# A decoder layer with a mixture of experts: the first expert's last token tile computed for all its tokens, and the down bias as one product of 72 stacked rows

## The reference

```python
logits = h @ router_weight.T + router_bias
top_vals, top_idx = jax.lax.top_k(logits, 2)
scores = zeros.at[token, top_idx].set(softmax(top_vals))        # T x 8
gate_up = einsum('th,ehj->etj', h, gate_up_proj) + gate_up_proj_bias
gate, up = minimum(gate_up[..., ::2], 7), clip(gate_up[..., 1::2], -7, 7)
act = (up + 1.0) * gate * sigmoid(1.702 * gate)
expert_out = einsum('eti,eih->eth', act, down_proj) + down_proj_bias
out = einsum('te,eth->th', scores, expert_out)
```

## Time and profile before

| what | value |
|---|---|
| median of 3 runs | 865.51 us (865.01 to 867.3) |
| profiled execution | 868.43 us, its span 866.6 us, mean granted clock 0.98 |
| PE busy | 840.4 us, 97% |
| DVE busy | 478.0 us, 55% |
| ACT busy | 319.1 us, 37% |
| POOL busy | 97.1 us, 11% |
| DMA | 97.39 MB, mean 112 GB/s |

### The profile page before, as it was taken

How to read it: one execution, slowest core, us unless ns; L and a number is a source line. 1 busy time by engine, 2 the same in 40 slices (tenths; PEclk the granted TensorE clock), 3 DMA queues, 4 the chain that set the end, 5 groups by cost and what they waited for, 6 DMA issues and landing times.

```text
span 866.6 us, 12600 instructions
## 1 busy us (share of the span) xinstructions
PE 840.4 (97%) x4913; PEld 735.6 (85%) x4913; DVE 478.0 (55%) x875; ACT 319.1 (37%) x718; POOL 97.1 (11%) x92
## 2 busy tenths in 40 slices
PE   7999999999999999999999999999988999999996
PEld 6989898989899898978799878888867888888883
DVE  4435445363635463485860343455576677777756
ACT  4443324242333433342352222122233365555434
POOL 0000000000000000000000000110221144443431
PEclk9999999999999999999999999999975999999998
DMA  9990634514030003003110001110287366665235
GB/s 326 341 283 20 204 132 143 189 56 147 6 98 6 25 8 122 1 6 133 50 36 1 4 33 36 61 49 13 63 327 222 126 201 182 190 197 156 53 68 182
DMA packets 35759, 97.39 MB, mean 112 GB/s; under 512 B 6665, under 2 KB 9225, under 8 KB 33009
## 3 DMA queue, kind: packets, MB, share of 16 engines
q1 hardware_dynamic: 32224, 88.69, 30.5%
q0 software_dynamic: 3472, 7.87, 4.5%
HBM read 64.10 MB, written 31.53 MB: 110 GB/s over the span
## 4 chain that ended last, share of the span: by engine, by line
PE 87%; DVE 6%; ACT 3%; issue 2%; DMA 1%; POOL 0%; POOLq 0%; SPq 0%; DVEq 0%
PE bank L315 69%; PE bank L696 3%; PE bank L730 3%; PE bank L625 3%; PE bank L789 2%; PE bank L684 1%; PE bank L1066 1%; DVE w_gu L1421 1%; DVE prob L1468 1%; PE bank L974 1%; PE bank L602 1%; PE bank L768 1%; PE bank L807 1%; ACT prob L1128 1%; DVE x_g L1421 1%
## 5 line engine op out<-in xcount | busy, mean ns | idle before, releaser
L315 PE MATMUL bank<-w_kv,cT 128*125 128x512 f32 x576 | 143.5, 400 | 0.0
L315 PE MATMUL bank<-xT,w_qkv 128*128 128x512 f32 (+1 forms) x672 | 137.8, 365 | 0.2 <-ACT qT L1118 0.2
L315 PEld LDWEIGHTS bank<-xT,w_qkv 128*128 128x128 f32 x672 | 122.1, 188 | 15.2 <-ACT qT L1118 0.5
L315 PEld LDWEIGHTS bank<-w_kv,cT 128*125 128x125 f32 x576 | 104.2, 186 | 23.7
L315 PE MATMUL bank<-x_g,w_gu 128*128 128x288 f32 x768 | 111.3, 304 | 3.4 <-DVE x_g L1421 2.9
L315 PEld LDWEIGHTS bank<-x_g,w_gu 128*128 128x128 f32 x768 | 107.2, 194 | 5.1 <-issue 3.2
L499 POOL TENSOR_TENSOR ln_rs<-ln_ve,half 128x1 f32<-128x1 f32 (+2 forms) x16 | 11.3, 710 | 629.3 <-DVE ln_ve L1550 614.8
L315 PE MATMUL bank<-w_o,zT 128*128 128x512 f32 x336 | 79.8, 395 | 0.5 <-DVE acc L1756 0.5
L315 PE MATMUL bank<-w_qkv,xT 128*128 128x256 f32 x588 | 77.3, 287 | 0.0
L315 PEld LDWEIGHTS bank<-w_o,zT 128*128 128x128 f32 x336 | 61.7, 188 | 15.0 <-DVE acc L1455 1.8
L315 PEld LDWEIGHTS bank<-w_qkv,xT 128*128 128x128 f32 x588 | 72.2, 191 | 0.0
(11 more groups left out here) (169 smaller groups left out, 1207.5 us busy)
## 6 DMA issues: line engine op xcount, KB each, us to landing
x_rows<-blank SPq DMA_DIRECT2D x9, 2084.0 KB, 16.1
raw_gu<-in_w_gu_dram SPq DMA_DIRECT2D x8, 2048.0 KB
raw_w<-in_w_qkv_dram SPq DMA_DIRECT2D x22, 512.0 KB, 8.6
raw_dn<-in_w_down_dram SPq DMA_DIRECT2D x8, 1024.0 KB, 8.9
raw_c<-in_ctx_t_dram SPq DMA_DIRECT2D x8, 750.0 KB, 4.3
raw_o<-in_w_o_dram SPq DMA_DIRECT2D x8, 512.0 KB, 4.4
xg<-x_rows SPq DMA_DIRECT2D x8, 512.0 KB, 6.7
raw_kv<-in_w_kv_dram SPq DMA_DIRECT2D x2, 1024.0 KB, 6.8
```

Source lines behind the costliest of these rows:

```text
L315: last = nc.tensor.matmul(mm_out, lhs(a, k), rhs(b, k), start=(k == 0 and i == 0), stop=(k == n - 1 and i == 2))
```

## The change

The last token tile (tile 6, `END`) does not send rows to expert 0 any more. Instead expert 0 is computed for all 128 tokens of this tile, token-wise on the partitions, and added with each token's score for expert 0 (zero where it didn't choose it). In the scatter, the slots of tile 6 that belong to expert 0 go to a part of `x_rows` that nobody reads, and tile 6 is not counted for expert 0. So expert 0's rows are complete after the scatter of tile 5, and SP reads them then; the load of `raw_gu[1]` stands behind that read, and the reads of experts 1 and 2 wait for the scatter of tile 6 (`end_out`).

The computation for tile 6 is: `end_gate_up`, three blocks of 8 products with 512 columns, for the three pairs of parts, each behind a piece of the old routing work, and two products of one row for the bias; `end_clamp`, `end_swish`, `end_hidden` on tiles of 128x512; `end_turn`, four transposes; `end_h_high`, `end_h_low`; `end_down`, 12 products of 512 columns, behind expert 0's gate/up; `end_add` into `acc`. `base_store(6)` waits for `end_add`.

With it the order of the experts changes: down of expert 0 now follows `end_down` directly, before gate/up of expert 1, and nothing stands between gate/up of experts 1 and 2. Expert 1's gate/up matrix is split wholly at the end of expert 0; expert 0's down matrix in its second and third quarter. `SPLITS` for expert 2's matrix is as before.

The down bias is one product a tile in place of three: scores are written three times in `score3` at rows 0, 32 and 64 of a 72-row stack, and the bias three times in `dn_b`, the middle one holding the low part of the bias and the last group of the scores the low part of the scores.

The rest of the diff merges semaphores (`bn_ok` into `mv_ok`, `ri_ok` into `rz_ok`, `level_ok` into `put_ok`, `rest_ok` into `made`, `id_ok` into `slot_ok`), with the same waits.

```diff
@@ banks and order of the last stretch
-            last = [("rk", 4), ("st", 0), ("t1", 5), ("rt", 5), ("t1", 6), ("rk", 5), ("rt", 6), ("db", 0), ("rk", 6),
-                    ("cnt", 0), ("db", 1), ("db", 2), ("st", 1), ("db", 3), ("db", 4), ("db", 5), ("db", 6)]
+            last = [("rk", 4), ("st", 0), ("t1", 5), ("rt", 5), ("db", 0), ("rk", 5), ("t1", 6), ("rt", 6), ("db", 1),
+                    ("rk", 6), ("st", 1), ("db", 2), ("db", 3), ("db", 4), ("db", 5), ("db", 6), ("cnt", 0)]
...
-        SPLITS = {0: ((3,), (), (), (), ()), 1: ((), (), (), (0,), (1, 2, 3))}
+        SPLITS = {0: ((), (), (), (), (0, 1, 2, 3)), 1: ((), (), (), (0,), (1, 2, 3))}
@@ SP
-            sp.wait_ge(*ready("wo", NT - 1))
-            sp.dma_start(raw_gu[1], t["w_gu"][1]).then_inc(in_gu[1], 16)
...
-            sp.wait_ge(row_out, 16 * 2 * NT)
-            for e in range(3):
+            sp.wait_ge(row_out, 16 * 2 * END)
+            rows_in(xg[0], 0, in_xg[0])
+            sp.wait_ge(*ready("wo", NT - 1))
+            sp.dma_start(raw_gu[1], t["w_gu"][1]).then_inc(in_gu[1], 16)
+            sp.wait_ge(end_out, 16 * 2)
+            for e in range(1, 3):
                 rows_in(xg[e], e * ROWS, in_xg[e])
@@ PE, last stretch
             cross_out(6)
             turn_x2(5)
             router(5)
+            down_bias(0)
+            rank(5)
             turn_x2(6)
-            rank(5)
             router(6)
-            down_bias(0)
+            end_gate_up(0, 0)
+            down_bias(1)
             rank(6)
-            count()
-            down_bias(1)
+            pe.wait_ge(m["end_dve"], 1)
+            end_gate_up(1, 0)
+            for h in range(2):
+                nc.tensor.matmul(banks[END_BANK[h]][:, :], all_ones[0:1, :], bias_end[0:1, h * D:(h + 1) * D], ...)
+            turn_scores(1)
             down_bias(2)
-            turn_scores(1)
-            for n in range(3, NT):
-                down_bias(n)
+            down_bias(3)
+            down_bias(4)
+            down_bias(5)
+            pe.wait_ge(m["gu_lo"], KC)
+            end_gate_up(0, 1).then_inc(m["end_mm"], 1)
...
-            for k in range(3):
-                gather(0, k)
+            gather(0, 0)
+            gather(0, 1)
+            down_bias(6)
+            count()
+            gather(0, 2)
@@ PE, experts
                     gate_up_part(e, w_gu[e % 2], x_g[e % 2], q)
-                    if e == 0 and q + 1 < KC:
-                        gather(1, q)
-                    if q and e and e + 1 < NE:
+                    if e == 0 and q == 0:
+                        end_turn()
+                        for k in (4, 5, 7):
+                            pe.wait_ge(free[k], LAST[k])
+                    if q and e + 1 < NE:
                         gather(e + 1, q - 1)
                 if e == 0:
-                    for k in range(6, 8):
-                        pe.wait_ge(free[k], LAST[k])
-                else:
+                    end_down()
+                if e != 1:
                     for k in range(3):
-                        down(e - 1, k)
+                        down(max(e - 1, 0), k)
@@ DVE, last stretch (new order)
+            choose(5)
             x2_norm(6)
-            choose(5)
             assign(5)
+            bias_add(0)
             choose(6)
+            split_lo(x_end[:, 1], x2T[:, END % 2], x_end[:, 0]).then_inc(m["end_dve"], 1)
             assign(6)
+            gu_low(0, 0, 0)
             bias_add(1)
-            gu_low(0, 0, 0)
+            gu_low(0, 0, 1)
             scores_low(1)
+            gu_low(0, 0, 2)
+            gu_low(0, 0, 3)
             bias_add(2)
...
+            gather_low(0, 0)
+            gather_low(0, 1)
+            bias_add(3)
+            gather_low(0, 2)
+            end_clamp()
+            bias_add(4)
+            end_hidden()
             bias_add(5)
             bias_add(6)
-            for k in range(3):
-                gu_low(1, 1, k)
+            levels()
@@ DVE, experts
-                    if q == 1 and not more:
+                    if q == 1 and not more or q == 2 and e == 0:
                         dn_low(e, e % 2)
                 hidden(e, KC - 1)
...
                 for k in splits_at(e, KC):
                     gu_low(e + 1, (e + 1) % 2, k)
+                    if e == 0 and k == 1:
+                        end_add()
-                if more:
+                if e and more:
                     dn_low(e, e % 2)
```

More of the change, by code:

```diff
@@ L423, in _ @@
             sp.dma_start(raw_gu[0], t["w_gu"][0]).then_inc(in_gu[0], 16)
+            with nc.allow_non_contiguous_dma(reason="one expert's bias as a row"):
+                sp.dma_start(bias_end[0:1, :].rearrange("o (c p) -> o c p", p=P),
+                             t["gu_b"].rearrange("p e c -> e c p")[0:1]).then_inc(in_bias, 16)
             sp.dma_start(raw_dn[0], t["w_down"][0]).then_inc(in_dn[0], 16)
@@ L1710, in _ @@
                 .then_inc(m["gub_ok"], 1)
+            nc.vector.memset(score3[:, :, :], 0.0)
             nc.vector.memset(csum[:, 0, :], 0.0).then_inc(m["csum_ok"], 1)
@@ L1736, in _ @@
             wo_low(p)
+            dve.wait_ge(m["wo_lo"], NP_)
+            nc.vector.memset(raw_dnb, 0.0).then_inc(m["ones_col"], 1)
             divide(p)
@@ L1857, in _ @@
             cross_stats(6)
+            choose(5)
             x2_norm(6)
[L1859 removed]
             assign(5)
+            bias_add(0)
             choose(6)
+            dve.wait_ge(m["end_act"], 1)
+            split_lo(x_end[:, 1], x2T[:, END % 2], x_end[:, 0]).then_inc(m["end_dve"], 1)
             assign(6)
[L1863 to L1865 removed]
@@ L1874, in _, with levels @@
             bias_add(1)
-            gu_low(0, 0, 0)
+            gu_low(0, 0, 1)
             scores_low(1)
+            gu_low(0, 0, 2)
+            gu_low(0, 0, 3)
             bias_add(2)
-            gu_low(0, 0, 1)
-            bias_add(3)
-            gu_low(0, 0, 2)
-            bias_add(4)
-            gu_low(0, 0, 3)
+            def levels():
+                dve.wait_ge(*ready("cnt", 0))
+                nc.vector.tensor_reduce(most[:, 0:1], bank("cnt", 0)[:, 0:NE], AX.X, ALU.max)\
+                    .then_inc(done("cnt", 0)[0], 1)
+                dve.wait_ge(*done("cnt", 0))
+                for j in range(ROUNDS - 1):
+                    nc.vector.tensor_scalar(most[:, j + 1:j + 2], most[:, 0:1], float((j + 1) * CAP), None, ALU.is_gt)\
+                        .then_inc(m["put_ok"], 1)
+                dve.wait_ge(m["put_ok"], 3 * NT + ROUNDS - 1)
+                nc.vector.tensor_reduce(most[:, 4:5], most[:, 1:4], AX.X, ALU.add).then_inc(m["put_ok"], 1)
+                dve.wait_ge(m["put_ok"], 3 * NT + ROUNDS)
+                nc.vector.tensor_copy(more_i[:, :], most[:, 4:5]).then_inc(m["more_ok"], 1)
@@ new lines, in end_h_low, with end_add @@
+            def end_h_low():
+                dve.wait_ge(m["end_act"], 3)
+                split_lo(h_end[:, 1], banks[6][:, :].rearrange("p (k c) -> p k c", k=KC), h_end[:, 0])\
+                    .then_inc(m["end_dve"], 1)
+            def end_add():
+                dve.wait_ge(m["end_mm"], 3)
+                dve.wait_ge(*done("db", END))
+                nc.vector.scalar_tensor_tensor(acc[:, END, :], banks[0][:, :], row[:, END, D:D + 1], acc[:, END, :],
+                                               ALU.mult, ALU.add).then_inc(m["end_dve"], 1)
```

224 lines of the change are left out of this document (144 added, 80 removed).

## The result

The changed kernel takes 885.19 us (median of 4 runs, 884.11 to 890.04), the kernel before, timed beside it, 866.40: ratio 1.0225, interval 1.0205 to 1.0245, **slower**. Predicted were 884.9. The profiled execution took 885.38 (span 883.4) against 868.43, so 16.95 us are to be found in the trace.

A forecast was written before the change was run, and what follows sets the result against it. PE, busy 97% of the span, was taken as the bound: its waits, granted clock and work. Terms up to gate/up 2's start summed to +19.4 us, 887.8 profiled, 884.9 as median; own range 880 to 890, overall 873 to 890.

The forecast's parts named there:

- The rows' wait: Ahead of expert 0's gate/up: rows land at about 653.5 instead of 658.35, some 5 us early; compute is late next.
- First gate/up product: Expert 0's start after the new work in the gap: 666.2, between 663.5 and 668.1, 4.0 later than 662.22.
- Expert 0's gate/up: Takes 16.7 us as with the old clock, between 15.3 and 17.2, ending at 682.9.
- Down of expert 0: Directly behind expert 0's gate/up: starts 7.0 us after it, PE idle some 3.7, then takes 9.5, to 699.4.
- Gate/up 1: Gate/up of expert 1 takes 13.9 us (14.30 without the last 0.36), to 713.3.
- The pause: Ahead of gate/up of expert 2, nothing covers the split of w_gu[0]: PE idles 9.4 us less 0.36 of transposes.
- The clock behind it: After the pause before gate/up 2 the clock is low: 24 products take 5.57 against 3.28, 2.3 us more.
- Sum: Start of gate/up 2 at 725.0 instead of 705.57, +19.4 us; 887.8 profiled, 884.9 as median.
- case 2: 128-row products raise the clock at the first block, or it never falls: +10.3 or +14.2, 876 to 880; chance 0.29.
- Cases 3 and 5: Case 3: expert 0's rows land at 668, 892.6 us, chance 0.05; case 5: clock never falls, split ready, 860.8, 0.04.
- case 4: Wait for w_gu[2] before gate/up 2 is covered though nothing on PE stands there: 11.7 off, 873.2; chance 0.10.
- The rule of the Trainium skill: Busy-ness releases PE's throttled clock; by it new products raise the clock early, as in case 2; the trace disagreed.

The follow-up runs named there:

- e11: Changed kernel with only the bias row's load moved behind both raw down loads; one run, 883.61 us.
- e7: e6 with expert 0's down-weight split ahead of the rows' gathers and the bias row's load behind the second raw down load; 876.36 us, 1.0119.
- e1: Changed kernel with down of expert 0 back between gate/up of experts 1 and 2; 883.77 us, 1.0208 times before.
- e5: Changed kernel with base_store(6) behind the load of expert 2's gate/up weights and their split moved whole to the end of expert 0; 880.65 us, 1.0159.
- e6: e5 with expert 2's rows transposed and split after quarters 0, 1 and 2 of expert 1; 878.82 us, 1.0148.
- e9: e8 with the splits of the next expert's rows (experts 0 and 1) ahead of each quarter's clamp and sigmoid; 866.43 us, 1.0007.
- e3: Kernel before with the stacked down bias alone, one product of 72 rows a tile instead of three of 8; 866.70 us, 1.001.
- e4: Kernel before with the 21 down bias products made of 128-row operands instead of 8, same count and columns; one run, 865.54 us.
- e8: e7 with the last tile's block reordered: first gate/up low parts before tile 6's levels, scores and down-bias products after the rows' transposes; 868.52 us, 1.0023.
- e12: e9 with the down-weight splits of experts 0 and 1 moved into idle time of DVE; 868.05 us, 1.0016.
- e10: e9 with the bias-row products in PE's two router waits and expert 0's down split behind the first quarter's hidden values; 872.45 us, 1.0067.

## Why the prediction was right

By its steps, each against the trace after.
- **The rows' wait goes, and compute is late next.** As said: no transfer is waited for. Expert 0's rows were asked for at 647.97 and 648.39, and no such read took over 5.3 us, so they lay there by 653.7 (653.5).
- **First gate/up product** 666.62, predicted 666.2, but partly by terms that cancel. The block's first eight products took 3.57 and ended at 648.62 (649.0). The clock rose at 649.3, fell at 656.2, rose at 663.0 and fell at 666.4; I had taken the middle of always low and always high without saying that it would go up and down. The bias products took 1.98, not 0.86: one-row products of full float32 take 0.48 each, and the trace has four for the two that the program writes. And the load of the bias row, costed at nothing, put router 5 0.6 late (e11).
- **Expert 0's gate/up** 15.6 (666.62 to 682.2), predicted 16.7: the first 24 products ran at 0.65, not 0.54, and took 4.58, not 5.57.
- **Down of expert 0** started 6.85 behind it (7.0), with 3.3 idle (3.7), half by the pushed split, as argued; e7 removed just that half. Down took 8.42, not 9.5: the clock stayed at 1.00 through two waits of 1.65. That term was mis-sized by 1.1.
- **Gate/up 1** 13.7 (13.9). **The pause** 9.04 idle, 9.4 with the transposes (9.4). e1 shows that it belongs to the cover, e5, e6 and e9 take it apart: the weights' splits (9.04 - 3.69 = 5.35), the rows' transposes (3.69 - 2.40 = 1.3), the place of the last split (2.40).
- **The clock behind it** 8.32 - 6.56 = 1.8 (2.3). That a pause of PE is paid twice holds for this one, not for each: 1.77 us of wait ahead of expert 1's gate/up brought 8.15 in the earlier trace rows and 6.64 in e3, and 2.40 brought 8.05 in e6 and 6.64 in e7.
- **Sum**: 720.69 + 1.76 = 722.45, and 722.45 - 705.57 = 16.9; predicted +19.4, too much by the 1.1 of gate/up 0, the 1.1 of down and some small ones. Against the profiled runs (16.95 apart) that is 2.5 too much, against the medians (885.19 - 866.40 = 18.8) 0.6, so the forecast of the median came out nearer than its terms deserve. The luck lies in the profiled runs: that of the kernel before was one of its longer ones, 2.0 above the median, that of the changed kernel lies 0.2 above its own.
- **The range.** Its upper end is said to hold a tenth more on each wait, but the sum has 7.6 and 9.8 for 7.0 and 9.4, less than a tenth; nothing hung on it.

The rivals: case 2 (clock early, 876 to 880) was half right, the block's 128-row products did bring the clock up, but it went down again in PE's own waits. Cases 3 and 5 did not occur; case 4 is excluded by the 9.04 row. The rule of the Trainium skill (TensorE: Matmul & The Clock Gate, What's actually happening) needs the reading that e4 gives: at the same busy time it was the 128-row products that came with the upper level, the 8-row ones did not, with the values of the operands not told apart from their rows.

## What to carry to other kernels

Before an order is changed to bring one operand early, list what the displaced work covered: here down of expert 0 hid a 9 us chain of splits and a load, and each came back as a wait. Read the queue of the engine ahead of a late split: much of the loss was place in an order, not cost (8.0 us came back by e8, 2.4 by e9, 1.65 by e7). Even mended, the change is worth nothing: e9 starts its first gate/up product 3.4 us before does, and by expert 3's gate/up (728.82 against 728.42) it has given it back. The last tile's own four transposes and twelve down products, new work on PE, take 3.3 us of that. Its waits (0.49, 1.37 and 1.70, the last two probably for a load that had lost its cover, e12) are 1.3 more than the 1.77 and 0.53 of the earlier trace rows. The slow clock costs both 3 to 4 us, at different places.

## What the hardware showed that I had not expected

- 4 KB in pieces of 4 bytes: 12.9 us from issue to the end of the wait for it (e10), and a 2 MB load issued just ahead of it came 2.5 us later in the changed kernel than in e11, 1.3 to 2.5 over five traces.
- A product of one row in full float32, 512 columns, takes 0.48 us at the upper level (651.57 to 653.48 for four) and 1.04 at the lower (e10), while a 128-row product in the split form takes 0.235 at the upper.
- The clock stayed at 1.00 through two PE waits of 1.65 us with 12 products between (684.38 to 689.05), but fell at 656.2, 0.3 us into a wait of 1.66 that followed one of 0.69; from 651.57 to there PE had run four products of one row, four of 72 and three transposes. What decides between the two was not tried.
- The same wait does not always bring the clock down. Behind 2.40 us of PE idle 48 gate/up products took 8.05 in e6, 6.64 in e7 and 6.62 in e8; behind 1.77 us they took 8.15 in the kernel before and 6.64 in e3. One and a half microseconds between two profiled executions can be this and no effect of an edit.
